# Routing batch 0 inside the last heads of a sandwich of attention and mixture of experts

## The chip, the cores and the metric

The kernel runs on 1 core of one Trainium2 chip. The metric is the device time of one execution in microseconds; a lower number is better. The core has TensorE (matmuls, written PE), VectorE (DVE), ScalarE (ACT), GpSimd (POOL) and SyncE (SP), which runs no arithmetic here and issues most DMA transfers. The engines run their own instruction streams in order and wait for each other by semaphores.

## The reference

Two layers with residuals. The input is x of 2 batches, 1024 tokens, width 128.

```python
x = x + layernorm(attention(layernorm(x)))
x = x + layernorm(moe(layernorm(x)))

# attention: 16 heads of 64, causal, relative bias clipped at 127 steps,
# logits / 64, softmax, out @ Wo + bo
# moe, over N = 2048 tokens:
shared = new_gelu(xf @ Wfc_s + bfc_s) @ Wproj_s + bproj_s      # 128 -> 512 -> 128
probs = softmax(xf @ Wr)                                       # 8 experts
topk_p, topk_i = top_k(probs, 2); topk_p /= sum(topk_p)
routed = sum over e of (new_gelu(xf @ Wfc[e] + bfc[e]) @ Wproj[e] + bproj[e]) * gate[:, e]
out = shared + routed
```

## The kernel before

Tokens lie in 16 blocks of 128 (blocks 0 to 7 are batch 0, 8 to 15 batch 1). Matrices enter TensorE split into a high and a low part, and a product is three matmuls (`three`, L1369 to L1371).

**Attention.** One head has S = 16 slots, one for each block of queries: slots 0 to 7 are batch 0, slots 8 to 15 batch 1. Such a half head is called a unit here. In a slot, TensorE computes scores (L1461), VectorE adds the bias and takes the row minimum (L1071), ScalarE takes the exponential (L817), two slots later TensorE transposes the probabilities into one of two banks trans_ps (L1476), ScalarE copies the high part out (L838), VectorE subtracts the low part (L1084). Products with V (L1494) and the output weights (L1508) are filled in at slots set by PV_SLOT and WO_SLOT. VectorE scales the head's result (`scale_head`, L1102), GpSimd adds it to `acc` (`add_head`, L626). Every engine runs `slot` for 16 slots of each head: head 0 written out, heads 1 to 14 as a loop (`Fori(1, H - 1)`), head 15 written out, and then the slots from S to TAIL that finish it. In slots GpSimd also splits the projection weights of the next head (`split_wqk`), splits V, and prepares one half of an expert's weights per head (`split_half`, stored by SyncE to `split_scratch`).

**Behind attention.** For each batch of 8 blocks: moments of `acc` (`moments`), an inverse root (`root` on GpSimd, three Newton steps on VectorE), the residual sum (`add_normed`), moments again, normalising on ScalarE (`normalise_moe_in`), transposes and evacuation (`nT_evac`), router logits, exponential, the choice of two experts (`choose`), the rank of every token within its expert by matmuls with a triangle of ones (`ranks`), and slot numbers (`find_slots`). With these GpSimd scatters each token's row (its 128 values, its gate, its number) twice into `rows_scratch`: `dispatch(b)` issues 16 indirect transfers for a batch, one per block and choice. `find_tiles` makes the table of 23 tiles of 256 rows. SyncE waits for the table, loads the first four tiles' weights, waits for all scatters (`dispatched`), and loads rows. TensorE meanwhile works on the shared expert: `hidden_units(0, c, 0)` and `second_layer(0, c, 0)` for four column groups c, in blocks of 12 wide matmuls, then `turn_shared`. Then the tiles follow (`tile_in`, `tile_units`, `tile_second`, `tile_result`), each result scattered by GpSimd, and last the sums, the layer norm and the output.

## Time and profile before

| | us |
|---|---|
| median of 3 runs | 793.9 (791.12 to 797.13) |
| the profiled execution, its own time | 788.15 |
| its span | 786.4 |
| busy: TensorE, VectorE, ScalarE, GpSimd | 697.0, 626.8, 551.9, 336.6 |

The page cuts the span into 40 slices and gives each engine's busy share in tenths. The timeline gives single instructions in order of time, with the idle time ahead of one and what ended it in brackets; "remote" and "issue" there mean that the profile shows no releaser. Times in the text are microseconds from the start of this span. The part of the span up to about 60 us loads and projects, attention runs from there to about 582, the routing and the shared expert to about 670, the tiles to about 760, the end sums to 786.

### The profile page before, as it was taken

How to read it: one execution, taken by the hardware profiler on the slowest of the kernel's cores; microseconds unless marked ns; L12 is line 12 of the kernel's file. 1: busy time of each engine (PE TensorE's matmuls, PEld its weight loads, DVE VectorE, ACT ScalarE, POOL GpSimd, SP SyncE). 2: the span in 40 equal slices, each digit the busy share in tenths (PEclk: the TensorE clock that was granted, in tenths of full speed). 3: DMA queues.
4: the chain of work that ended last, by engine and by line, in shares of the span. 5: the costliest groups of instructions: out<-in, count | busy, mean ns of one | idle time of the engine just before them, and what ended most of it. 6: DMA issues, size and time to landing. Idle time of an engine off the chain costs nothing.

```text
span 786.4 us, 17200 instructions
## 1 busy us (share of the span) xinstructions
PE 697.0 (89%) x4466; PEld 614.5 (78%) x4466; DVE 626.8 (80%) x1663; ACT 551.9 (70%) x1305; POOL 336.6 (43%) x417
## 2 busy tenths in 40 slices
PE   5978999999999999999999999999976566899930
PEld 4857888888888888888888888888875444899920
DVE  5648888889888898888988888888888615688837
ACT  2437888788887888888888888878724414888823
POOL 2518864243432434334343343333343770156544
PEclk9979999999999999999999999999997677999985
DMA  8683653546436465364553645536300246599823
GB/s 297 240 301 79 162 137 83 152 86 170 131 73 161 89 158 137 67 164 93 151 137 72 158 98 146 137 80 157 105 2 1 60 145 212 196 354 370 287 84 110
DMA packets 81474, 114.85 MB, mean 146 GB/s; under 512 B 42432, under 2 KB 59328, under 8 KB 79008
## 3 DMA queue, kind: packets, MB, share of 16 engines
q1 hardware_dynamic: 78656, 108.71, 49.6%
q0 software_dynamic: 2496, 5.15, 1.8%
q10 hardware_dynamic: 288, 0.59, 0.3%
q8 instruction: 14, 0.23, 0.1%
q14 instruction: 20, 0.16, 0.1%
HBM read 48.32 MB, written 32.56 MB: 103 GB/s over the span
## 4 chain that ended last, share of the span: by engine, by line
PE 72%; DVE 9%; issue 6%; DMA 3%; POOL 3%; another core or an unknown queue 3%; ACT 3%; SPq 0%; ACTq 0%; POOLq 0%; DVEq 0%
PE out_ps L1494 17%; PE score_ps L1461 16%; PE trans_ps L1476 16%; PE shared_ps L1508 7%; PE shared_ps L1369 2%; DVE pT_lo L1316 2%; PE shared_ps L1371 2%; PE shared_ps L1370 2%; PE score_ps L1371 2%; PE score_ps L1369 2%; PE score_ps L1370 1%; PE out_ps L1410 1%; DMA v_scratch<-probs 1%; PE trans_ps L1369 1%
## 5 line engine op out<-in xcount | busy, mean ns | idle before, releaser
L817 ACT ACTIVATE probs<-score_ps,row_min 128x128 f32<-128x128 f32 (+7 forms) x256 | 189.8, 742 | 54.1 <-DVE row_min L1071 54.0
L1084 DVE TENSOR_TENSOR pT_lo<-trans_ps,pT_hi 128x512 fp32r<-128x512 f32 (+3 forms) x384 | 201.6, 552 | 17.1 <-ACT pT_hi L838 17.0
L838 ACT ACTIVATE pT_hi<-trans_ps 128x512 fp32r<-128x512 f32 (+3 forms) x384 | 185.0, 491 | 41.2 <-PE trans_ps L1476 29.4
L1071 DVE CUSTOM_DVE_ANT_0 score_ps<-score_ps,bias 128x128 f32<-128x128 f32 (+7 forms) x256 | 194.7, 760 | 22.4 <-PE score_ps L1461 19.2
L1476 PE MATMUL trans_ps<-ident,probs 128*128 128x128 f32 x1152 | 190.9, 275 | 2.3 <-DVE pT_lo L1084 1.6
L1461 PE MATMUL score_ps<-k_hl,q_hl 128*128 128x512 f32 (+2 forms) x768 | 184.3, 354 | 2.4 <-DMA k_hl<-k_hl 1.3
L626 POOL TENSOR_TENSOR acc<-acc,head_out 128x512 f32<-128x512 f32 x64 | 83.1, 1298 | 215.9 <-DVE head_out L1102 215.8
L1476 PEld LDWEIGHTS trans_ps<-ident,probs 128*128 128x128 f32 x1152 | 137.3, 140 | 26.6 <-DVE pT_lo L1084 12.2
L1494 PE MATMUL out_ps<-pT_hi,v_hl 128*128 128x512 f32 (+2 forms) x384 | 156.5, 409 | 1.1 <-DVE pT_lo L1084 1.1
L1461 PEld LDWEIGHTS score_ps<-k_hl,q_hl 128*128 128x128 f32 x768 | 135.8, 190 | 23.4 <-issue 2.0
L1494 PE MATMUL out_ps<-pT_lo,v_hl 128*128 128x512 f32 (+2 forms) x384 | 133.0, 347 | 0.0
L1494 PEld LDWEIGHTS out_ps<-pT_hi,v_hl 128*128 128x128 f32 x384 | 72.7, 189 | 5.5 <-DVE pT_lo L1084 1.3
L1494 PEld LDWEIGHTS out_ps<-pT_lo,v_hl 128*128 128x128 f32 x384 | 73.3, 191 | 4.4
L1508 PE MATMUL shared_ps<-wo,oT 128*128 (+1 forms) x512 | 70.0, 275 | 0.8 <-ACT oT L846 0.8
L1508 PEld LDWEIGHTS shared_ps<-wo,oT 128*128 128x128 f32 x512 | 65.7, 191 | 3.5 <-issue 1.0
L1028 DVE TENSOR_TENSOR k_hl<-shared_ps,k_hl 128x512 fp32r<-128x512 f32 x64 | 44.2, 691 | 28.2 <-ACT k_hl L781 28.2
L612 POOL CAST v_hl<-v_raw 128x512 fp32r<-128x512 f32 x32 | 19.6, 611 | 90.6 <-PE out_ps L1494 69.1
L817 ACT ACTIVATION_READ_ACCUMULATOR probs<-score_ps,row_min 128x1 f32 x256 | 51.9, 203 | 0.0
L1316 DVE TENSOR_TENSOR pT_lo<-probs,pT_hi 128x256 fp32r<-128x256 f32 x92 | 38.9, 424 | 11.7 <-issue 4.6
L958 ACT ACTIVATE probs<-score_ps,tile_bias 128x256 f32<-128x256 f32 x92 | 41.9, 475 | 7.9 <-PE score_ps L1371 4.9
L1102 DVE TENSOR_TENSOR head_out<-shared_ps,row_inv 128x512 f32<-128x512 f32 x64 | 42.3, 661 | 1.1 <-PE shared_ps L1508 1.0
L614 POOL TENSOR_TENSOR v_hl<-v_raw,v_hl 128x512 fp32r<-128x512 f32 x32 | 41.1, 1284 | 2.7
(246 smaller groups left out, 1177.2 us busy)
## 6 DMA issues: line engine op xcount, KB each, us to landing
q_hl<-k_hl SPq DMA_DIRECT2D x64, 256.0 KB, 3.7
k_hl<-k_hl SPq DMA_DIRECT2D x32, 512.0 KB, 4.5
v_scratch<-probs SPq DMA_DIRECT2D x16, 512.0 KB, 4.2
v_raw<-v_scratch SPq DMA_DIRECT2D x32, 256.0 KB, 4.1
split_scratch<-normed_rows SPq DMA_DIRECT2D x16, 512.0 KB, 5.3
k_hl<-split_scratch SPq DMA_DIRECT2D x16, 512.0 KB
rows_scratch<-wv SPq DMA_DIRECT2D x16, 455.0 KB, 6.3
normed_rows<-in_W_halves SPq DMA_DIRECT2D x16, 256.0 KB, 3.8
```

The costliest lines, as they stand in the source:

```text
L626: pool.tensor_tensor(acc[:, blocks, :], acc[:, blocks, :], head_out[c][:].rearrange("p (t d) -> p t d", d=D), ALU.add)\
L817: act.activation(probs[s % 4][:, 0:n], scores_of(s % QB)[:, 0:n], ACT.Exp, bias=row_min[:, s:s + 1], scale=-1.0, accum_out=row_sum[:, s:s ...
L838: act.activation(pT_hi[c][:, CH * g:CH * g + m, q * P:(q + 1) * P], trans_ps[k % 2][:, 0:m * P].rearrange("p (m q) -> p m q", q=P), ACT.Co ...
L1028: dve.tensor_tensor(k_hl[b][:, 1, cols], shared_ps[:], k_hl[b][:, 0, cols], ALU.subtract).then_inc(qk_lo, 1)
L1071: dve.tensor_tensor_reduce(out=ps, in0=ps, in1=bias_b[b][:, T - n:T], scale=1.0, scalar=3e38, op0=ALU.add, op1=ALU.min, accum_out=row_min[ ...
L1084: dve.tensor_tensor(pT_lo[c][dst], trans_ps[k % 2][:, 0:m * P].rearrange("p (m q) -> p m q", q=P), pT_hi[c][dst], ALU.subtract).then_inc(p ...
L1102: dve.tensor_tensor(head_out[c][:].rearrange("p (t d) -> p t d", d=D), shared_ps[:].rearrange("p (t d) -> p t d", d=D), row_inv[:, blocks] ...
L1316: dve.tensor_tensor(lo, raw, hi, ALU.subtract).then_inc(tile_lo, 1)
L1461: last = pe.matmul(scores_of(i)[:, at:end], q, k_hl[b][:, part, at:end], start=part == 0, stop=part == 1)
L1476: last = pe.transpose(trans_ps[k % 2][:, o:o + P], probs[s % 4][:, j * P:(j + 1) * P], ident[:])
L1494: last = pe.matmul(out_ps[:, q0:W], v_hl[b][:, j, :], part[c][:, j, q0:W], start=j == 0 and part is pT_hi, stop=j == nk - 1 and part is pT_lo)
L1508: last = pe.matmul(shared_ps[:, j * P:(j + 1) * P], oT[c][:, j * P:(j + 1) * P], wo[:, h, :], start=True, stop=True)
```

## The change

The first eight heads stay as they are (both batches in a head). The last eight are taken batch by batch: loop heads 8 to 11 run batch 0 of heads 8 to 15, two in each, and loop heads 12 to 15 run batch 1 of them (`unit`). So batch 0's attention is complete when loop head 12 begins, and its routing is laid into the 64 slots of loop heads 12 to 15 by a function `route_early(z)` on each engine, z being the slot 0 to 63. Heads 7 to 15 are now written out instead of looped. 13 of batch 0's 16 scatters stand in slots 55 to 63, the other 3 right behind the last slot. Batch 1 is routed behind attention in two groups, blocks 8 to 11 and 12 to 15 (PICKS). The projection weights are split once for each unit of the last eight heads. The shared expert's weights become two more of the halves that are split in the heads (18 instead of 16; two heads take two), and are loaded once in the last head. Two blocks of shared hidden units are moved ahead of batch 1's routing. Tokens are numbered by partition first, which makes the loads of tile rows (1040 bytes a piece instead of 520) and of the results (2048 instead of 512) longer pieces.

```diff
+    LAST = 8
+    F = H - LAST
+    P0 = F + LAST // B
+    TWICE = (F + 1, F + 2)
+    SCATTERS = {55: 1, 56: 2, 57: 2, 59: 1, 60: 2, 61: 2, 62: 2, 63: 1}
+    EARLY = sum(SCATTERS.values()) - QB
+    PICKS = [(0, QB), (QB, QB + CH), (QB + CH, NB)]
...
+    def unit(h, b):
+        if isinstance(h, int) and h >= F:
+            i = B * (h - F) + b
+            return F + i % LAST, i // LAST
+        return h, b
...
+            # GpSimd
+            def add_residual(c):
+                blocks = slice(CH * c, CH * (c + 1))
+                pool.wait_ge(std_ready, c + 1)
+                then_wait(pool.tensor_tensor(acc[:, blocks, :], acc[:, blocks, :],
+                                             rstd[:, blocks].unsqueeze(2).broadcast_to([P, CH, D]), ALU.mult))
+                pool.tensor_tensor(x_sb[:, blocks, :], x_sb[:, blocks, :], acc[:, blocks, :], ALU.add).then_inc(residual_added, 1)
...
+                if z in (10, 11):
+                    root(1, CH * (z - 10), CH * (z - 9))
+                if z in (14, 15):
+                    add_residual(z - 14)
+                if z in (18, 19):
+                    root(2, CH * (z - 18), CH * (z - 17))
+                if z == 24:
+                    name_rows(0)
...
+                for n in range(SCATTERS.get(z, 0)):
+                    k = sum(m for y, m in SCATTERS.items() if y < z) + n
+                    dispatch(0, k // QB, k % QB)
...
-            with pool.Fori(1, H - 1) as h:
+            with pool.Fori(1, F - 1) as h:
                 for s in range(S):
                     slot(h, s, True, False)
-            for s in range(S):
-                slot(H - 1, s, True, True)
+            for h in range(F - 1, H):
+                for s in range(S):
+                    slot(h, s, True, h == H - 1)
...
+            # ScalarE
+                if 22 <= z < 22 + QB:
+                    normalise_moe_in(z - 22, z - 21)
+                if z in (29, 37):
+                    nT_evac(1, (z - 29) // 8)
+                if z == 46:
+                    exp_logits(0)
...
-            exp_logits(0)
-            normalise_moe_in(1)
-            for c in range(NC, NCH):
-                nT_evac(1, c)
+            hidden_units(0, 0)
+            normalise_moe_in(QB, QB + CH)
+            nT_evac(1, NC)
+            act.wait_ge(moe_in_ready, QB + CH)
             copy_rows(1)
             exp_logits(1)
-            hidden_units(0, 0)
+            normalise_moe_in(QB + CH, NB)
+            nT_evac(1, NC + 1)
+            act.wait_ge(moe_in_ready, NB)
+            copy_rows(2)
+            exp_logits(2)
             hidden_units(0, 1)
...
+            # VectorE
+                if z in (9, 10):
+                    lo = CH * (z - 9)
+                    if z == 9:
+                        dve.wait_ge(acc_added, P0 * B * NC)
+                    moments(acc, lo, lo + CH)
+                if z in (12, 13):
+                    lo = CH * (z - 12)
+                    stand(lo, lo + CH).then_inc(std_ready, 1)
+                if z in (17, 18):
+                    lo = CH * (z - 17)
+                    dve.wait_ge(residual_added, z - 16)
+                    moments(x_sb, lo, lo + CH)
+                if z in (20, 21):
+                    lo = CH * (z - 20)
+                    scale_and_offset(2, lo, lo + CH)
+                if z == 24:
+                    make_order()
+                if z in (29, 37):
+                    nT_evac(1, (z - 29) // 8)
+                if z == 45:
+                    take_logits(0)
+                if z in (47, 49):
+                    choose(0, (z - 47) // 2)
+                if z == 51:
+                    share(0)
+                if z == 53:
+                    find_slots(0)
...
+            # TensorE
+                if z in (28, 36):
+                    wait_shared(h, s, last)
+                    transposes(1, (z - 28) // 8)
+                if z in (30, 38):
+                    pe.wait_ge(nT_ready, NCH + 1 + (z - 30) // 8)
+                if z == 44:
+                    wait_shared(h, s, last)
+                    logits(0)
+                if z == 46:
+                    pe.wait_ge(logit_ready, 1)
+                if z == 52:
+                    wait_shared(h, s, last)
+                    ranks(0)
+                if z == 54:
+                    pe.wait_ge(ranks_taken, 1)
...
-            keep_busy(56)
-            for c in range(NC):
-                transposes(1, c)
-            pe.wait_ge(wo_scaled, H * B * NC)
-            pe.wait_ge(nT_ready, NCH + NC)
-            logits(0)
-            pe.wait_ge(wfc_ready, 1)
-            hidden_units(0, 0, 0)
+            hidden_units(0, 1, 0)
+            keep_busy(24, trans_ps[1])
+            transposes(1, NC)
+            pe.wait_ge(nT_ready, NCH + NC + 1)
+            logits(1)
+            transposes(1, NC + 1)
+            ranks(1)
+            pe.wait_ge(nT_ready, 2 * NCH)
+            logits(2)
             keep_busy(16, trans_ps[0])
-            ranks(0)
-            for c in range(NC, NCH):
-                transposes(1, c)
-            pe.wait_ge(nT_ready, 2 * NCH)
-            logits(1)
-            ranks(1)
-            hidden_units(0, 1, 0)
+            ranks(2)
             second_layer(0, 0, 0)
```

The comments that name an engine are added here. `hidden_units(0, 0, 0)` now stands on TensorE in slot 18 of the last head, ahead of the last products with V.

**GpSimd from the end of the last head to the tiles.** `rstd<-var_eps,minus_half` is `root`, `rows_scratch<-` are scatters. Before, behind the last `split_half` and `move_empty`:

```order
L559 TENSOR_SCALAR normed_rows<-normed_rows 128x2
L626 TENSOR_TENSOR acc<-acc,head_out 128x512
L712 TENSOR_SCALAR normed_rows<-token 128x16
L712 TENSOR_SCALAR bias_all<-token 128x16
L736 CAST wqk_hl<-wr 128x8
L737 TENSOR_TENSOR wqk_hl<-wr,wqk_hl 128x8
L577 TENSOR_TENSOR rstd<-var_eps,minus_half 128x8
L626 TENSOR_TENSOR acc<-acc,head_out 128x512 x2
L577 TENSOR_TENSOR rstd<-var_eps,minus_half 128x8 x2
```

Then four rows that split the shared weights, one more root, and the scatters:

```order
L577 TENSOR_TENSOR rstd<-var_eps,minus_half 128x8
L724 DMA rows_scratch<-normed_rows,slot_u 18432x130 x8
L724 DMA rows_scratch<-bias_all,slot_u 18432x130 x8
L724 DMA rows_scratch<-normed_rows,slot_u 18432x130 x8
L724 DMA rows_scratch<-bias_all,slot_u 18432x130 x8
```

Now, the part in the last head and right behind it:

```order
L693 DMA rows_scratch<-wqk,slot_u 18432x130 x5
L603 CAST normed_rows<-normed_rows 128x512
L606 TENSOR_TENSOR normed_rows<-normed_rows 128x512
L661 TENSOR_TENSOR acc<-acc,head_out 128x512
L593 TENSOR_SCALAR wv<-wv 128x7
L593 TENSOR_SCALAR normed_rows<-normed_rows 128x2
L693 DMA rows_scratch<-wqk,slot_u 18432x130 x3
L693 DMA rows_scratch<-bias_all,slot_u 18432x130 x4
L661 TENSOR_TENSOR acc<-acc,head_out 128x512
L693 DMA rows_scratch<-bias_all,slot_u 18432x130 x4
L661 TENSOR_TENSOR acc<-acc,head_out 128x512
L611 TENSOR_TENSOR rstd<-var_eps,minus_half 128x4
```

and behind the last statistics:

```order
L661 TENSOR_TENSOR acc<-acc,head_out 128x512
L611 TENSOR_TENSOR rstd<-var_eps,minus_half 128x4
L671 TENSOR_SCALAR normed_rows<-token 128x8
L671 TENSOR_SCALAR bias_all<-token 128x8
L611 TENSOR_TENSOR rstd<-var_eps,minus_half 128x4 x2
L693 DMA rows_scratch<-normed_rows,slot_u 18432x130 x4
L693 DMA rows_scratch<-bias_all,slot_u 18432x130 x4
L693 DMA rows_scratch<-normed_rows,slot_u 18432x130 x4
L693 DMA rows_scratch<-bias_all,slot_u 18432x130 x4
```

16 of 32 scatters have moved ahead of GpSimd's last two additions, 13 of them into the slots, and 16 stand behind the last roots.

**VectorE in slots 3 to 6 of the last head** (z = 51 to 54). L1071 and L1145 are the row minimum with its read-out, L1084 and L1158 the low part of the transposed probabilities. Before:

```order
L1102 TENSOR_TENSOR head_out<-shared_ps,row_inv 128x512
L1071 ISA score_ps,row_min<-score_ps,bias 128x640
L1071 ISA row_min 128x1
L1084 TENSOR_TENSOR pT_lo<-trans_ps,pT_hi 128x3x128
L1071 ISA score_ps,row_min<-score_ps,bias 128x768
L1071 ISA row_min 128x1
L1084 TENSOR_TENSOR pT_lo<-trans_ps,pT_hi 128x4x128
L1071 ISA score_ps,row_min<-score_ps,bias 128x896
L1071 ISA row_min 128x1
L1084 TENSOR_TENSOR pT_lo<-trans_ps,pT_hi 128x4x128
```

Now, from slot 5 on:

```order
L1145 ISA score_ps,row_min<-score_ps,bias 128x768
L1145 ISA row_min 128x1
L1158 TENSOR_TENSOR pT_lo<-trans_ps,pT_hi 128x4x128
L1268 SCALAR_TENSOR_TENSOR place<-count,shared_ps 128x64
L1274 TENSOR_TENSOR place_of<-place,pick 128x64
L1275 TENSOR_REDUCE slot_f<-place_of 128x8
L1276 CAST slot_u<-slot_f 128x8
L1274 TENSOR_TENSOR place_of<-place,pick 128x64
L1275 TENSOR_REDUCE slot_f<-place_of 128x8
L1276 CAST slot_u<-slot_f 128x8
L1145 ISA score_ps,row_min<-score_ps,bias 128x896
L1145 ISA row_min 128x1
```

The seven rows of `find_slots(0)` stand between the subtraction of slot 5 and the row minimum of slot 6. Eleven more such insertions stand in earlier slots of the last four heads.

## Rows read from the trace of the kernel before

**Rows 1.** The page: busy tenths of TensorE and GpSimd in 40 slices of the span.
```profile
PE   5978999999999999999999999999976566899930
...
POOL 2518864243432434334343343333343770156544
```

**Rows 2.** Stages: window us, busy us (instructions) by engine, clock, DMA share, GB/s.
```profile
476.00:508.50 32.50, 32.49 (x215) 28.83 (x213) 28.70 (x69) 26.96 (x65) 12.64 (x17) 1.00 0.50 123
...
587.00:609.70 22.70, 13.70 (x79) 11.62 (x77) 19.23 (x97) 9.96 (x23) 8.64 (x7) 0.77 0.00 1
...
626.00:655.00 29.00, 13.85 (x36) 9.36 (x36) 4.92 (x10) 3.63 (x7) 18.98 (x20) 0.73 0.41 124
655.00:670.50 15.50, 13.02 (x52) 9.76 (x52) 11.72 (x30) 9.62 (x18) 0.00 (x0) 0.84 0.87 282
670.50:750.00 79.50, 75.97 (x618) 73.39 (x619) 65.86 (x196) 66.14 (x181) 38.85 (x38) 1.00 0.84 293
```

**Rows 3.** Timeline in one head: start us, us, engine line op, shapes, [idle before <-releaser].
```profile
484.59 0.69 DVE L1084 TENSOR_TENSOR pT_lo<-trans_ps,pT_hi 128x512 fp32r<-128x512 f32 x1
...
485.40 0.60 PE L1476 MATMUL trans_ps<-ident,probs 128*128 128x128 f32 x4
...
485.75 1.10 DVE L1071 CUSTOM_DVE_ANT_0 score_ps<-score_ps,bias 128x896 f32<-128x896 f32 x1 [0.46 <-PE score_ps L1461]
```

**Rows 4.** Timeline of GpSimd: the first and the last of 32 scatters.
```profile
609.71 1.25 POOL L724 DMA_INDIRECT rows_scratch<-normed_rows,slot_u  x1 [7.35 <-DVE slot_u L1248]
...
649.82 0.95 POOL L724 DMA_INDIRECT rows_scratch<-bias_all,slot_u  x1 [0.30 <-issue]
```

**Rows 5.** Timelines of ScalarE, SyncE and TensorE during the scatters.
```profile
621.89 0.69 ACT L913 ACTIVATE probs<-score_ps,layer_bias_T 128x512 f32<-128x512 f32 x1 [2.04 <-PE score_ps L1371]
626.10 0.69 ACT L913 ACTIVATE probs<-score_ps,layer_bias_T 128x512 f32<-128x512 f32 x1 [3.52 <-PE score_ps L1371]
...
632.43 0.69 ACT L913 ACTIVATE probs<-score_ps,layer_bias_T 128x512 f32<-128x512 f32 x1 [5.13 <-remote]
...
654.99 1.26 ACT L913 ACTIVATE probs<-score_ps,layer_bias_T 128x512 f32<-128x512 f32 x2 [15.05 <-remote]
...
628.78 3.52 SPq L476 DMA_DIRECT2D k_hl<-split_scratch  x2
...
650.56 0.59 PE L1371 MATMUL trans_ps<-pT_hi 128*128 128x512 f32 x1 [2.41 <-issue]
```

**Rows 6.** Timeline of TensorE behind attention.
```profile
580.93 1.13 PE L1508 MATMUL shared_ps<-wo,oT 128*128 128x128 f32 x8 [0.78 <-ACT oT L846]
...
601.87 0.43 PE L1369 MATMUL score_ps<-nT_hi,pT_hi 128*128 128x512 f32 x1
...
604.70 1.91 PE L1410 MATMUL trans_ps<-ident 128*128 128x128 f32 x16
...
606.93 0.92 PE L1612 MATMUL shared_ps<-taken,ones 128*128 128x56 f32 x7
...
619.86 0.77 PE L1369 MATMUL score_ps<-nT_hi,pT_hi 128*128 128x512 f32 x1
...
670.54 0.41 PE L1639 MATMUL out_ps<-ident,wqk 128*128 128x128 f32 x2 [0.29 <-ACT acc L936]
```

**Rows 7.** Timeline of VectorE: moments, inverse root, and first and last routing operation.
```profile
777.14 0.87 DVE L999 BATCH_NORM_STATS2 stats<-acc 128x6 f32<-128x128 f32 x4
...
778.46 0.17 DVE L1004 TENSOR_SCALAR var_eps<-mv 128x4 f32<-128x4 f32 x1
...
775.13 0.15 DVE L1010 TENSOR_TENSOR newton<-rstd 128x4 f32<-128x4 f32 x1
...
775.74 0.16 DVE L1145 SCALAR_TENSOR_TENSOR offset<-mv,rstd 128x4 f32<-128x4 f32 x1
...
603.69 0.21 DVE L1218 TENSOR_REDUCE top<-rank 128x8 f32<-128x64 f32 x1
...
609.24 0.17 DVE L1248 CAST slot_u<-slot_f 128x8 uint32<-128x8 f32 x1
```

563 lines of the change are left out of this document (308 added, 255 removed).

## The prediction

> **What bounds the kernel now.** I read the page first. TensorE is busy in every slice of the attention stretch and thins out to 5 to 8 tenths in slices 30 to 35; in slices 32 and 33 GpSimd, little used in attention, is busier than TensorE [rows 1]. The table by stage says it in numbers: a head takes 32.50 us, TensorE is busy for all of it and VectorE for 28.70, so VectorE has 3.8 us to spare per head. Behind attention TensorE is half idle: from 587 to 609.7 VectorE is the busiest engine, from 626 to 655 no compute engine is; from 655 to 670.5 TensorE catches up, and from 670.5 on run the 23 expert tiles, where it is full again [rows 2].
>
> Next the timelines. In a head, the transposes of one slot start at 485.40, just 0.12 us after VectorE's subtraction of two groups earlier ends (484.59 + 0.69); TensorE's transposes take turns in two banks that VectorE frees. VectorE itself then waits 0.46 us for scores [rows 3]. So the two engines pull on each other, and work given to VectorE in such slots soon comes out at TensorE.
>
> Behind attention GpSimd issues 32 scatters of rows, one each 1.265 us, from 609.71 to past 649.82 [rows 4]. In the last two thirds of them the others crawl: a gelu at 621.89 is still in time, the next ones come at 626.10 and 632.43, and after one more (6.3 us on) at 654.99; SyncE needs 3.5 us to issue two transfers; TensorE stands 2.41 us between two matmuls of one sum, which wait for nobody [rows 5]. All recover once the scatters have ended. The shared expert's matmuls are what is late: the first transpose of the first tile is at 670.54 [rows 6].
>
> **The change part by part.** The sum is made against the profiled execution: 788.15 us, of which the span is 786.4. It lies 5.75 us below the median of the runs, 793.9, and I carry that difference over.
>
> *Added to attention.* The routing of batch 0 now runs in the slots of the last four heads. On VectorE it is: moments of four blocks (777.14 to 778.63, say 1.4 us) four times, the inverse root with its last product (775.13 to 775.90, say 0.8) four times, and about 0.8 us of small operations for the order, 9.6 us together in slots 9 to 24. Then two evacuations of 0.65 us in slots 29 and 37. Then 0.9 us for the logits, four operations like those in the row of 603.69, and 5.7 us from the first choice to the last slot number (603.69 to 609.41), 6.6 us in slots 45 to 53 [rows 7]. Each of the three clusters is covered only by VectorE's spare time in its own slots. Of the 3.8 us per 16 slots I count 0.8 as usable, since part of it is wait for a neighbour [rows 2, 3]: 9.6 less 3.0, 1.3 less 0.9, and 6.6 less 1.8, together about 12. TensorE itself gets 8 transposes, 16 narrow matmuls and 8 more for the ranks, about 4 us at the 0.12 us that its narrow matmuls take (seven in 0.92) [rows 6]; 3 of these stand beside the third cluster, 1 adds. The attention stretch grows by 13 us. The bounds are 5 (if the slack of two slots by which the softmax runs ahead takes up most) and 18 (if no spare time is usable and TensorE's 4 us add).
>
> Nothing is charged for the rest. ScalarE gets 8 normalisations (about 0.4 us each) and two copies in 27 slots and has 5.5 us to spare per head; GpSimd's extra splits of the projection weights and its two residual additions stand in 19.9 us of spare time per head [rows 2]. If GpSimd were late, the values' matmuls would wait next. The shared weights cost one load in the last head instead of a load and four operations behind it, which were hidden.
>
> *The scatters.* 13 of batch 0's 16 stand in slots 55 to 63, 3 right behind. That is 16.5 us in about 18 us, and GpSimd has some 5 us of other work there, so it runs late by 3 to 4 us, and its last addition but one is needed about 8 us behind the last slot: just covered. By the Trainium skill (SBUF — State Buffer, Who interferes with whom) a scatter of GpSimd's is held up while VectorE runs a two-port operation, from about 0.62 to 3.1 us in its example. The rows of the tile stage, where VectorE is busy for 65.86 of 79.5 us, have 38 scatters in 38.85 us, 1.02 each [rows 2], which is as long as the row of 649.82, where VectorE idles [rows 4]; with the pitch I take 1.265.
>
> *Behind attention.* I walk the new order with the same durations, in times of the profile of before, without the 13 us. One block of shared hidden units goes ahead of the last values, so the last output product moves from 580.93 to 582.4 [rows 6]. Batch 1 goes in groups of four blocks: statistics of group 1 at 582, its sum at 586.6, the second statistics at 589.4, normalised by ScalarE at 593.8, turned and evacuated at 596.5, logits at 598.6, exponential at 600.2 (ScalarE now has to load its table twice more, because gelu goes ahead). Group 2's normalisation is queued behind that exponential and its evacuation ahead of group 1's choice: choice at 604.2 to 607.2, the slots of group 1 at 612 (before, batch 0's were ready at 609.4). Group 2 chooses until 615, has its slots at 617.5 and the tile table at 621. GpSimd scatters 16 times from 612: 20.2 us, to 632, against 650.8 before [rows 4]. TensorE's remaining six blocks wait for VectorE, which splits the first hidden units only behind the table, about 624. A block of 12 wide matmuls took 2.83 us at a granted clock of 1.00 (601.87 to 604.70) and 5.1 at half clock (from 619.86) [rows 6]. One at 4.4 and five at 2.9 with 0.8 us between them end at 644; four turns of 0.7 us, 647; and 2.5 us for slow issue late in the 16 scatters (it began about 12 us into the 32). The first tile starts at 649.5 instead of 670.5: 21 us earlier. Bounds: 14 (the chain of group 1 is 7 us longer) and 27 (no slow issue, full clock). The tiles take the 91 us that they took. Rows are now loaded and summed in longer pieces, for which I take 1.5 us off the end, between 0 and 3.
>
> **Sum.** +13 - 21 - 1.5 = -9.5: profiled 778.7, and 784.4 beside the median.
>
> **Rivals.**
> - *A, the slots absorb it.* If the softmax's lead of two slots hides the clusters, attention grows by 5 to 7 us: 793.9 + 6 - 21 - 1.5 = 777.5. For it: the first clusters stand just behind the first slots of a batch, where blocks are short. Against: the margin of 0.12 us [rows 3].
> - *B, batch 1's own chain is long.* Two groups cost two passes over each wait, and ScalarE's order (hidden units, normalise, exponential, normalise) puts group 2 behind group 1. If the first scatter of batch 1 is 7 to 10 us later than I have it, the tiles start only 12 us earlier: 793.9 + 13 - 12 - 1.5 = 793.4, no change. For it: every one of some 20 hand-overs between engines in this chain is counted here at its bare duration.
> - *C, the scatters stop the last head; slower.* In before, slow issue set in about 12 us into an unbroken run of scatters [rows 5]. In the last head TensorE needs over six matmuls per us, so slow issue there is a full stop. If it sets in from the tenth scatter, 7.6 us are lost (6 x 1.265): 792. If from the first, 20 us: 804.6, slower. It decides at about 9.5 us lost. Against: 38 scatters in the tile stage at a like density stop nobody [rows 2].
> - *D, VectorE holds the scatters up.* If each of the 16 waits for one more of VectorE's operations of about 1.1 us [rows 3], 17.6 us are added ahead of the last two additions, of which some 14 are on the path: 798. The skill's rule (named above) goes this way; at its 3.1 us for each scatter the same sum would be over 805. The trace so far speaks against it.
>
> **How the numbers follow.** My forecast has 0.50, A 0.20, B 0.16, C 0.10, D 0.04. The predicted time is the likeliest, 784.4; its own range is 778 to 790. The whole range, 773 to 798, takes in A, B, and the milder part of C. About 1% is what a measurement of this kernel can tell from no change: 786.0 to 801.8. Of my own case six tenths lie below 786, A wholly, B hardly: faster 0.52. The rest of my case, B, and half of C: same 0.41. Slower 0.07.
>
> **What would show it.** In the profile of after: heads 8 to 11 keep 32.5 us; the last four are together 13 us longer than 130, with TensorE waiting for VectorE's pT_lo in slots 9 to 24 of them and 45 to 55; GpSimd's scatters last about 1.0 us with pitch 1.265 and TensorE isn't idle during them in the last head; from attention's last output product to the first tile about 67 us instead of 90; gelus 1.1 us apart except in the last few us of scatters. I am wrong if the last four heads grow by under 8 or over 18 us, if the span between attention and the first tile shrinks by under 15, or if the tile stage is longer because its weights come later against its start.

## Result, and the profile after

| | kernel before, us | changed kernel, us |
|---|---|---|
| median (7 runs each) | 793.9 (791.12 to 797.13) | 800.47 (798.72 to 803.4) |
| ratio of the medians | 1 | 1.0084, 95% interval 1.0062 to 1.0107 |
| the profiled execution, its span | 786.4 | 801.5 |
| first row minimum of loop head 2 | 116.8 | 117.8 |
| last output product | 580.93 | 609.64 |
| first tile | 670.54 | 677.63 |
| first to last tile | 73.9 | 81.7 |
| last tile to the end | 42.0 | 42.2 |

The change is slower by 0.8%. The forecast was 1.2% faster. From head 2 on, the way to the last output product grew by 27.8 us (491.9 against 464.1), the way from there to the first tile shrank by 21.6 us (68.0 against 89.6), and the tiles took 7.9 us longer in this one execution. The two profiled executions are no typical pair: that of the changed kernel (803.4) is 2.9 us above its median, that of the kernel before (788.15) 5.75 us below.

The page of the changed kernel, the rows that answer to [rows 1]: TensorE's thin stretch is four slices (31 to 34) instead of six (30 to 35), but slices 24, 25 and 28 to 30, in and right behind the last heads, show eights, and GpSimd's peak is split in two, one at the end of attention and one ahead of the tiles.

```profile
PE   4967999999999999999999988998887557989830
POOL 2418853343343442444434364443284170345444
```

Stages of the changed kernel, with the columns of [rows 2]: loop heads 11 to 15, the way from the last row minimum to the last output product, and the way from there to the first tile.

```profile
411.49:444.18 32.69, 32.51 (x213) 28.84 (x213) 28.96 (x69) 26.84 (x64) 13.33 (x18) 1.00 0.51 125
444.18:480.49 36.31, 33.39 (x213) 28.86 (x213) 32.80 (x95) 26.93 (x64) 18.05 (x24) 1.00 0.53 129
480.49:519.43 38.94, 34.26 (x217) 29.11 (x217) 33.84 (x106) 30.31 (x73) 18.17 (x24) 1.00 0.42 103
519.43:558.71 39.28, 36.63 (x242) 32.31 (x241) 32.61 (x81) 29.03 (x68) 15.93 (x21) 1.00 0.43 105
558.71:592.57 33.86, 30.14 (x183) 25.69 (x184) 29.51 (x80) 22.18 (x55) 14.41 (x16) 0.95 0.33 99
592.57:609.64 17.07, 13.46 (x74) 11.30 (x74) 6.70 (x15) 6.14 (x13) 11.92 (x12) 0.90 0.18 58
609.64:677.63 67.99, 41.36 (x184) 32.33 (x184) 43.63 (x170) 27.34 (x49) 21.72 (x23) 0.75 0.35 112
```

The same three last stages of the kernel before:

```profile
539.22:569.07 29.85, 28.75 (x185) 24.87 (x185) 25.13 (x62) 23.32 (x57) 9.65 (x11) 1.00 0.39 106
569.07:580.93 11.86, 9.15 (x61) 7.84 (x62) 9.34 (x30) 5.71 (x12) 4.79 (x7) 1.00 0.06 18
580.93:670.54 89.61, 56.85 (x259) 45.06 (x259) 52.14 (x206) 30.17 (x57) 41.86 (x41) 0.75 0.31 98
```

Heads 12 to 15 are 3.8, 6.4, 6.8 and 4.0 us longer (against 32.50 and 29.85), 21.0 together. VectorE is busy 3.8, 4.9, 3.7 and 4.4 us longer in them (against 28.96 in loop head 11 and 25.13 in the last head of before), 16.8 together. The stretch behind the last row minimum is 5.2 us longer. Heads 7 to 11 add 1.5.

Who waited for whom in about one head of the kernel before (474 to 506 us; us in total, times, longest), and behind it the same in loop head 13 of the changed kernel:

```profile
ACT probs L817 <- DVE row_min L1071: 3.2, 6, 1.1
DVE k_hl L1028 <- ACT k_hl L781: 1.6, 4, 0.5
...
DVE score_ps L1071 <- PE score_ps L1461: 1.1, 3, 0.5
DVE pT_lo L1084 <- ACT pT_hi L838: 0.9, 4, 0.3
```

```profile
ACT probs L878 <- DVE row_min L1145: 7.5, 9, 2.6
...
PE score_ps L1583 <- ACT probs L878: 1.4, 1, 1.4
...
PE trans_ps L1598 <- DVE pT_lo L1158: 1.3, 2, 0.8
PE trans_ps L1598 <- ACT probs L878: 1.1, 2, 0.6
```

Before, VectorE's three waits for ScalarE and TensorE make 3.6 us, nearly all of its idle time. Now TensorE waits for VectorE mainly in two ways: directly for pT_lo (1.3 us), as the forecast had it, and over ScalarE (2.5 us), whose exponentials wait 7.5 us for late row minima.

The runs were made in seven groups, each on one chip with its own runs of the kernel before, and only kernels of one group are compared by time. The groups differ: in two of them (e1 to e4; e13 to e16) the kernel before took 773 us, in the other five 791 to 795. I call them the 773 groups and the 790 groups. The experiments show where those 20 us lie. "Slow issue" is what [rows 5] show: during a run of scatters the other engines stop for microseconds with no releaser in the profile.

### The profile page after: what moved, and what is told of

It reads as the page before. It is cut to its first block, busy times and chain, and to the rows that moved or that the text cites. A ratio compares the mean times of both kernels' runs of the same rounds, so it can differ in the third digit from the quotient of the medians.

```text
span 801.5 us, 15822 instructions
## 1 busy us (share of the span) xinstructions
PE 692.9 (86%) x4435; PEld 607.2 (76%) x4435; DVE 632.2 (79%) x1704; ACT 553.2 (69%) x1308; POOL 349.5 (44%) x444
## 4 chain that ended last, share of the span: by engine, by line
PE 66%; DVE 16%; ACT 5%; DMA 5%; issue 4%; POOL 3%; SPq 0%; another core or an unknown queue 0%; ACTq 0%; DVEq 0%; POOLq 0%
PE out_ps L1616 15%; PE trans_ps L1598 14%; PE score_ps L1583 13%; PE shared_ps L1630 6%; DVE score_ps L1145 2%; PE shared_ps L1489 2%; DMA v_scratch<-probs 2%; PE score_ps L1491 2%; PE trans_ps L1489 2%; DVE pT_lo L1158 2%; PE shared_ps L1491 2%; DVE pT_lo L1436 2%; PE shared_ps L1490 2%; PE score_ps L1489 2%; PE score_ps L1490 1%
## 5 line engine op out<-in xcount | busy, mean ns | idle before, releaser
L1158 DVE TENSOR_TENSOR pT_lo<-trans_ps,pT_hi 128x512 fp32r<-128x512 f32 (+3 forms) x384 | 202.5, 553 | 22.6 <-ACT pT_hi L899 19.0
L1145 DVE CUSTOM_DVE_ANT_0 score_ps<-score_ps,bias 128x128 f32<-128x128 f32 (+7 forms) x256 | 194.6, 760 | 21.4 <-PE score_ps L1583 17.3
L1598 PEld LDWEIGHTS trans_ps<-ident,probs 128*128 128x128 f32 x1152 | 136.7, 141 | 42.2 <-issue 17.7
L1616 PEld LDWEIGHTS out_ps<-pT_lo,v_hl 128*128 128x128 f32 x384 | 73.9, 192 | 4.4
L1630 PE MATMUL shared_ps<-wo,oT 128*128 128x128 f32 (+1 forms) x512 | 70.0, 275 | 0.8 <-ACT oT L907 0.8
L1436 DVE TENSOR_TENSOR pT_lo<-probs,pT_hi 128x256 fp32r<-128x256 f32 x92 | 38.6, 424 | 19.8 <-ACT pT_hi L1025 11.3
L907 ACT ACTIVATE oT<-out_ps 128x512 f32<-128x512 f32 x64 | 38.4, 601 | 6.0 <-PE out_ps L1616 6.0
```

The source lines that it names most:

```text
L1145: dve.tensor_tensor_reduce(out=ps, in0=ps, in1=bias_b[b][:, T - n:T], scale=1.0, scalar=3e38, op0=ALU.add, op1=ALU.min, accum_out=row_min[ ...
L1158: dve.tensor_tensor(pT_lo[c][dst], trans_ps[k % 2][:, 0:m * P].rearrange("p (m q) -> p m q", q=P), pT_hi[c][dst], ALU.subtract).then_inc(p ...
L1436: dve.tensor_tensor(lo, raw, hi, ALU.subtract).then_inc(tile_lo, 1)
L1598: last = pe.transpose(trans_ps[k % 2][:, o:o + P], probs[s % 4][:, j * P:(j + 1) * P], ident[:])
L1616: last = pe.matmul(out_ps[:, q0:W], v_hl[b][:, j, :], part[c][:, j, q0:W], start=j == 0 and part is pT_hi, stop=j == nk - 1 and part is pT_lo)
L1630: last = pe.matmul(shared_ps[:, j * P:(j + 1) * P], oT[c][:, j * P:(j + 1) * P], wo[:, unit(h, b)[0], :], start=True, stop=True)
```

## Experiments

### Routing taken out of the slots

`e1_routed_behind` keeps the new order of heads. All pieces of `route_early` and the scatters run behind the last output product. One part of the result differs in it: the first block of shared hidden units is computed ahead of batch 0's normalised input, from the old operand; the work is the same.

```diff
-        return B * QB * (h - P0) + s if isinstance(h, int) and h >= P0 else -1
+        return -1
```

> The changed kernel with its new order of heads, but all of batch 0's routing and its 16 scatters stand behind the last output product instead of in the slots. In the profile of the changed kernel the last output product starts at 609.64 us (before: 580.93); by head, heads 12 to 15 grew by 21.0 us, heads 8 to 11 by 1.4. Theory (the growth is the routing laid into the slots): heads 12 to 14 fall back to 32.5 each, the last product starts at 587 (within 2 us), and only the moved block of hidden units (3.9 us) and 1 to 2 us of heads 8 to 11 are left of the growth. Rival (written-out heads or the order batch by batch cost by themselves): heads 12 to 14 stay above 34 each and the last product starts past 595. The routing is then serial: about 27 us of it come behind attention, so the time is 805 to 815 by the theory.

Measured: last product at 586.58, time 815.9 (ratio 1.0569 to the kernel before), just past the top of the 805 to 815 expected. Heads 12 to 14 take 32.7 to 32.9 and head 15 takes 29.82:

```profile
445.20:477.90 32.70, 32.51 (x213) 28.84 (x213) 28.93 (x69) 26.87 (x64) 13.34 (x18) 1.00 0.51 124
...
543.46:573.28 29.82, 28.71 (x185) 24.85 (x185) 25.17 (x61) 23.33 (x57) 9.67 (x11) 1.00 0.45 131
573.28:586.58 13.30, 11.70 (x73) 10.04 (x74) 6.11 (x12) 5.72 (x12) 2.55 (x2) 1.00 0.01 2
```

So all but 0.7 of the 21 us in heads 12 to 15 are the routing in the slots, and neither written-out heads nor the order batch by batch. (e2 below, of the same group and with the routing in the slots, has 149.6 us in these four heads, e1 128.1.) Those leave 1.6 us in heads 7 to 11, and the hidden block leaves 1.4 (13.30 against 11.86).

### What a microsecond in a slot costs

`e3_price_list` and `e8_price_list_2` are the kernel before, heads written out, with one extra piece of work in single heads.

```diff
+                n = {(2 + i, i): 6 for i in range(QB)}.get((h, s), 0)
+                if h == 14 and s % QB in (2, 3, 4):
+                    n = 3
+                for t in range(n):
+                    last = dve.bn_stats(stats[:, t, :], x_sb[:, t, :])
```

> The kernel before with all heads written out and one extra piece in single heads: six bn_stats of 128x128 on VectorE (0.22 us each, 1.3 us) behind slot i of head 2 + i, for i = 0 to 7; sixteen narrow matmuls on TensorE in slot 12 of head 11; eight transposes in slot 12 of head 13; eighteen bn_stats in threes behind slots 2, 3, 4, 10, 11, 12 of head 14; nothing extra in heads 1, 10, 12. Period of a head without extra: 32.5. Theory (margins of the two transpose banks: 0.1 to 0.3 us for blocks 5, 6, 7, 0, 1 and 1.4 to 1.8 for blocks 2 to 4, two slots behind their row minimum): 1.3 us cost 1.0 to 1.3 where the margin is narrow and 0 to 0.3 behind slots 3 to 5, the spread ones cost under 1.5 of 3.9; TensorE's pieces cost all they last, 3.6 to 4.0 for the narrow matmuls (0.25 each) and 2.1 for the transposes (0.27 each). Rival (the lead of the softmax hides pieces of this size): every VectorE piece costs under 0.4, the narrow matmuls about 2, as taken in the forecast (0.12 each).

> The kernel before with all heads written out (32.68 us each without extra) and one extra piece in single heads: ScalarE three copies of 128x128 in slot 1 of head 2 and one in each of slots 1 to 6 of head 4; GpSimd eight products of 128x128 in slot 4 of head 6 (about 0.46 us each); VectorE thirteen dependent products of 128x64 in slot 1 of head 8 (about 3.3 us), two bn_stats in slot 6 of head 12 (0.45 us), twelve bn_stats in slot 1 of head 14 (2.7 us). In the first list 1.35 us of bn_stats cost 0.85 to 1.6 and eighteen spread ones (4.05 us) 3.4. Theory (in a head TensorE and VectorE are one chain without usable slack, ScalarE and GpSimd have some): VectorE's pieces cost 0.3 to 0.5, 2.5 to 3.0 and 3.0 to 3.4; ScalarE's cost under 0.5 and under 1.0, GpSimd's under 0.5. Rival (every engine that hands over between slots is as tight): ScalarE's 1.2 and 2.4 us cost 1.0 and 2.0.

Some heads of e3: the first two without extra (10, 12), then head 2 (six bn_stats behind slot 0), head 11 (sixteen narrow matmuls), head 13 (eight transposes) and head 14 (eighteen bn_stats, spread). The first number is the period of the head.

```profile
389.12:421.80 32.68, 32.50 (x213) 28.82 (x213) 28.95 (x69) 26.89 (x64) 12.61 (x16) 1.00 0.51 125
...
456.53:489.22 32.69, 32.51 (x213) 28.82 (x213) 28.95 (x69) 26.91 (x64) 12.66 (x16) 1.00 0.46 112
```

```profile
118.16:152.33 34.17, 32.81 (x213) 28.72 (x213) 30.30 (x75) 27.19 (x64) 12.64 (x16) 1.00 0.48 119
...
421.80:456.53 34.73, 34.54 (x229) 30.49 (x229) 28.96 (x69) 27.01 (x64) 12.64 (x16) 1.00 0.51 128
...
489.22:522.80 33.58, 33.39 (x222) 29.60 (x221) 28.89 (x70) 27.01 (x64) 12.62 (x16) 1.00 0.52 128
522.80:558.86 36.06, 34.37 (x213) 28.70 (x213) 32.37 (x88) 26.59 (x64) 12.61 (x16) 1.00 0.47 116
```

And of e8: head 4 (six copies on ScalarE), head 6 (eight products on GpSimd), head 8 (thirteen dependent products on VectorE).

```profile
183.48:216.55 33.07, 32.62 (x213) 28.65 (x212) 28.89 (x69) 28.13 (x70) 12.56 (x16) 1.00 0.52 131
249.23:282.22 32.99, 32.80 (x214) 28.97 (x214) 28.88 (x70) 27.05 (x65) 15.78 (x24) 1.00 0.51 125
314.82:350.78 35.96, 33.13 (x214) 28.73 (x214) 31.79 (x83) 26.73 (x64) 12.62 (x16) 1.00 0.46 113
```

| extra piece | its length, us | head longer by, us |
|---|---|---|
| VectorE, 6 bn_stats behind slot 0, 1, ... 7 | 1.35 | 1.5, 1.6, 1.2, 1.2, 0.9, 1.0, 1.2, 1.0 |
| VectorE, 18 bn_stats spread over six slots | about 4 (3.4 more busy) | 3.4 |
| VectorE, 2 bn_stats; 12 bn_stats; 13 dependent products | 0.4; 2.4; 2.9 more busy | 0.35; 2.4; 3.3 |
| TensorE, 16 narrow matmuls; 8 transposes | 2.0; 0.9 more busy | 2.05; 0.9 |
| ScalarE, 3 copies in one slot; 6 in six slots | 0.7; 1.3 more busy | 0.0; 0.4 |
| GpSimd, 8 products of 128x128 | 3.1 more busy | 0.3 |

My theory of e3 was mostly wrong: the margins of single blocks don't matter, work behind slots 3 to 5 costs nearly as much as elsewhere (0.9 to 1.2), and TensorE's pieces cost half of what I expected. The rival, that the lead hides pieces of this size, is wrong for every piece on VectorE. A microsecond of VectorE costs 0.9 on average in the eight single places (0.6 to 1.2), and 0.8 to 1.1 in the other pieces, spread or not; ScalarE's costs a third at most, GpSimd's a tenth. Differences of 0.3 us are at the limit of this measurement: head 3 of e8, without an extra piece, is 0.26 us longer than the others too. TensorE's narrow matmuls cost 0.13 each, as the forecast had them.

`e10_small_ops_off` uses this in the changed kernel: the Newton steps, shift and offset of batch 0 run on GpSimd (`norm`, in slots 12 and 20), and so do the constants of the order.

```diff
-                if z in (12, 13):
-                    lo = CH * (z - 12)
-                    stand(lo, lo + CH).then_inc(std_ready, 1)
+                if z == 12:
+                    norm(1)
```

> The changed kernel with the Newton steps, the shift, the offset and the order's constants of batch 0 moved from VectorE (twelve to sixteen small operations in slots 12, 13, 20, 21 and 24 of the 64, 3.9 us in all) to GpSimd, which waits about 20 us per head. Theory (a us of VectorE in a slot costs 0.9 us, GpSimd's costs 0.04): loop head 12 shrinks from 36.3 by 1.0 to 1.6 us, head 13 from 38.9 by 1.8 to 2.4, together 3 to 4 us, and the last output product is as much earlier. Rival (what costs is the number of insertions and their waits, not their length): under 1.5 us in all.

```profile
445.01:480.14 35.13, 32.99 (x213) 28.74 (x213) 31.55 (x87) 26.88 (x64) 17.40 (x28) 1.00 0.54 133
480.14:517.83 37.69, 34.21 (x217) 29.07 (x217) 32.25 (x88) 30.01 (x74) 21.49 (x41) 1.00 0.43 104
```

Only 2.8 us left VectorE (32.80 to 31.55 and 33.84 to 32.25), less than the 3.9 I had counted; the two heads shrank by 2.4, 0.86 per microsecond, which is the price. The last head took 0.6 to 0.9 us more than in the other kernels (34.77 against 33.9 to 34.1); why is open. Time 797.6 (ratio 1.0049, 1.0017 to 1.0081, to the kernel before); this interval overlaps those of the changed kernel, so only the two heads show the gain.

### The scatters in the last head

`e2_scatters_out` and, in another group, `e11_scatters_out_2` put batch 0's 16 scatters behind the last roots.

```diff
+    SCATTERS = {}
...
-            for g in range(1, len(PICKS)):
+            for g in range(len(PICKS)):
```

> The changed kernel with batch 0's 16 scatters taken out of the last head and put where GpSimd waited 17 us for batch 1's slot numbers (behind its last roots). All the rest stays. Theory A (the cluster of VectorE and TensorE work makes the last head long, scatters cost little): last output product within 1.5 us of 609.6, last head 33 to 34 us. Theory B (scatters slow the others' issue in the last head too, as forecast rival C had it): last product 4 to 8 us earlier. In both, batch 1's scatters end near 661 us less what is won, with issue slow for up to 20 us ahead of that: 796 to 803.

> The kernel of e2_scatters_out again, since the two groups of runs differ by 18 us in the kernel before. From the last row minimum to the last output product the changed kernel took 17.1 and 18.2 us, e2_scatters_out 13.3. Theory (the scatters stop the last transposes and not the group of runs): 13.3 again, 4 to 5 us won in attention. Where slow issue is present it now falls into 32 scatters in a row: way from last product to first tile 75 us or more instead of 66.8, time 2 to 8 us longer than the changed kernel; where absent, 64 us.

| from last row minimum to last product, us | scatters in the last head | scatters out |
|---|---|---|
| 790 groups | 17.07 (changed kernel), 18.16 (e5), 15.38 (e10) | 13.31 (e11) |
| 773 groups | 13.30 (e15) | 13.30 (e2, and e1) |

In a 773 group the scatters cost nothing, in a 790 group 2 to 5 us (2.1 in e10, 3.8 and 4.9 in the changed kernel). ScalarE in the changed kernel, first profile, waiting for transposes; behind it the same in e15_changed_pauses (below), which has the same 16 scatters there:

```profile
596.75 0.60 ACT L899 ACTIVATE pT_hi<-trans_ps 128x512 fp32r<-128x512 f32 x1 [1.40 <-PE trans_ps L1598]
598.22 0.49 ACT L899 ACTIVATE pT_hi<-trans_ps 128x384 fp32r<-128x384 f32 x1 [0.88 <-remote]
601.03 0.60 ACT L899 ACTIVATE pT_hi<-trans_ps 128x512 fp32r<-128x512 f32 x1 [2.32 <-PE trans_ps L1598]
```

```profile
595.69 0.98 ACT L901 ACTIVATE pT_hi<-trans_ps 128x512 fp32r<-128x512 f32 x2
597.82 1.09 ACT L901 ACTIVATE pT_hi<-trans_ps 128x512 fp32r<-128x512 f32 x2 [1.16 <-PE trans_ps L1600]
```

In a 790 group the scatters cost more outside the head than in it: e11 has its first tile 77.8 us behind the last product (changed kernel 66.8 to 68.0) and takes 807.1 us, ratio 1.0154 (1.010 to 1.0208). e2 has 64.3 us and takes 787.6 against 773.4, ratio 1.0182 (the 796 to 803 expected were for a 790 group). Its last product is at 608.5, as theory A had it; e11's 13.31 against 17.07 shows theory B where slow issue is present.

### The two kinds of groups, the layout, the hidden block

> The changed kernel itself, on the chip of this group. The first profiles had the change at plus 28.7 us up to the last output product, minus 21.6 from there to the first tile, plus 7.9 in the tiles. In the group of runs before this one the kernel before took 773.4 instead of 793.9, and with the new layout its way from last product to first tile was 74.0 us instead of 89.6, with no stretch of slow issue. Theory (the growth in attention is the same everywhere, the gain behind it depends on slow issue): on a chip where the kernel before takes about 773, the change is slower by 14 to 20 us, its last product is 28 us later and the way to the first tile only 6 to 10 us shorter. Rival (the change moves both chips alike): ratio 1.008, 5 to 8 us slower.

> The kernel before, for its profile on this chip. By the theory of slow issue as a property of the chip or its state: gelus during the 32 scatters at 0.57 us behind one another and no gap over 9 us where this chip gives 773 us; gaps of 5 to 15 us as in the first profile where it gives 794.

> The kernel before with the new numbering of tokens alone: rows of tiles loaded in pieces of 1040 bytes, results in pieces of 2048 bytes. In the profiles the 22 tile pitches sum to 73.86 us before and 81.73 after the change. Theory (the tile stage differs by chance from run to run): sum of pitches 74 to 76, time 0 to 2 us shorter than before. Rival (the longer pieces, or the order in which rows lie, slow the loads of weights): pitches 78 to 82, time 4 to 8 us longer.

`e4_layout_only` changes three places of the kernel before (token numbering and the two loads). It ran in a 773 group: 771.9 against 773.4, ratio 0.9995 (0.9973 to 1.0016). The layout is worth nothing. e5 and e6 met a 790 group, on the same chip as e1 to e4: changed 797.7, before 791.1, ratio 1.0082 (1.0064 to 1.010), the first result again. So e5 could not test its own theory; e2 and e15, in 773 groups, do (1.0182 and 1.0209).

| | last product to first tile, us | sum of tile pitches, us |
|---|---|---|
| before, 790 groups | 89.6 and 89.8 (e6) | 73.9, 75.1 |
| changed, 790 groups | 68.0 and 66.8 (e5) | 81.7, 74.5 |
| before, 773 groups | 74.0 (e4), 74.6 (e3) | 71.0, 72.8 |
| changed with edits, 773 groups | 64.3 (e2), 67.2 (e15) | 71.0, 70.2 |

So the kernel before loses 15.6 us here to slow issue (89.6 against 74.0), which only the 790 groups have. Without it the changed order is 6.8 us (e15, whose pauses lengthen it) to 9.7 us (e2) shorter than 74.0, so 12 to 15 of the 21.6 us that the change won behind attention are slow issue avoided. ScalarE between the scatters, e6 and then e4:

```profile
626.61 0.69 ACT L913 ACTIVATE probs<-score_ps,layer_bias_T 128x512 f32<-128x512 f32 x1 [3.56 <-PE score_ps L1371]
...
632.93 0.69 ACT L913 ACTIVATE probs<-score_ps,layer_bias_T 128x512 f32<-128x512 f32 x1 [5.12 <-remote]
...
656.18 1.27 ACT L913 ACTIVATE probs<-score_ps,layer_bias_T 128x512 f32<-128x512 f32 x2 [14.34 <-remote]
```

```profile
624.01 0.69 ACT L912 ACTIVATE probs<-score_ps,layer_bias_T 128x512 f32<-128x512 f32 x1 [0.59 <-PE score_ps L1370]
...
635.54 1.39 ACT L912 ACTIVATE probs<-score_ps,layer_bias_T 128x512 f32<-128x512 f32 x2 [8.13 <-PE score_ps L1370]
...
641.08 1.39 ACT L912 ACTIVATE probs<-score_ps,layer_bias_T 128x512 f32<-128x512 f32 x2 [1.44 <-PE score_ps L1370]
```

TensorE in the first profile of the kernel before, between two matmuls of the shared expert:

```profile
639.47 0.79 PE L1369 MATMUL score_ps<-nT_hi,pT_hi 128*128 128x512 f32 x1 [4.63 <-issue]
```

In that profile the queues that load instructions (kind instruction, q8 and q14 on the page) moved nothing from 610 to 665 us; nor did they in e6 from 611 to 667:

```profile
q1 hardware_dynamic: 2877, 4.99, 29.9%
q0 software_dynamic: 1024, 2.13, 11.4%
```

These are all queues with packets in that stretch, so a late load of instructions is not what stops the engines. What stops them is open.

The scatters themselves have the same pitch in both (1.265). In e4 the shared expert is done before the scatters end, and the first tile waits for its rows. The tiles of the two kinds differ too. TensorE, the DMA share and GB/s (last column) in 40 us of tiles, e6 and then e4:

```profile
695.00:735.00 40.00, 38.64 (x313) 37.01 (x312) 33.71 (x101) 32.23 (x89) 22.55 (x22) 1.00 1.03 362
```

```profile
680.00:720.00 40.00, 40.00 (x343) 40.00 (x342) 36.08 (x110) 36.54 (x99) 23.31 (x25) 1.00 1.04 397
```

`e7_hidden_block_back` moves `hidden_units(0, 0, 0)` behind the last output product.

> The changed kernel with the first block of shared hidden units back behind the last output product. Theory (the block stands in TensorE's way and pays nothing back where the scatters bound the start of the tiles): last product 3 to 4 us earlier, first tile 3 to 4 us earlier, time 3 to 4 us shorter than the changed kernel. Rival (TensorE waits there anyway for the last transposes): last product at most 1 us earlier, time the same or longer by the block.

The stretch behind the last row minimum is 16.5 us instead of 18.2 (e5, same group), the way to the first tile 66.3 instead of 66.8, the time 796.8 against 797.7: the block costs 1.5 us, not 3 to 4, and taking it out is no gain that this run can tell.

> The three edits together: small operations on GpSimd, batch 0's scatters behind the last roots, first hidden block behind the last product. Theory (they add up): last output product 3.5 + 4.5 + 1.5 = 9.5 us earlier than the changed kernel's, against e11 5 us earlier. Compared with the kernel before: plus 9 us where slow issue is absent (e2 was plus 14), and about plus 2 where it is present. Rival (they overlap): last product no more than 6 us earlier.

`e12_three_together` took 804.5 against e11's 807.1. The stretch behind the last row minimum fell to 11.86, exactly that of the kernel before, but heads 13 and 15 didn't shrink (39.2 and 35.1). From head 2 to the last product it took 487.3, against 488.7 in e11: 1.4 us, not 5. The edits don't add up, and against the kernel before e12 is 11.4 us slower, where I had expected 2. Why head 15 grew is open.

### Pauses between the scatters

All four kinds are the kernel before, but for e15, with something behind some scatters:

```diff
                         pool.indirect_dma_start(...)
+                        if t % 4 == 3 and (b, i, t) != (1, 1, NB - 1):
+                            then_wait(pool.tensor_scalar(head_out[0][:], head_out[0][:], 1.0, None, ALU.mult))
```

That is e9. e13 and e17 do the same on 4 columns instead of 512, e14 and e18 the long one behind every eighth scatter, e16 waits there for all scatters so far instead, and e15 has the long one behind every fourth of batch 1's 16.

> The kernel before with one operation of GpSimd on 128x512 (about 1.3 us, its result unused) behind every fourth of the 32 scatters, seven in all. Slow issue was there in the groups of runs where the kernel before took 791 and 794 us, and absent where it took 773. Theory A (an unbroken run of scatters brings slow issue on): with pauses it goes away or starts later, gelus stay under 3 us apart, the scatters end 9 us later, and where slow issue is present the first tile starts 5 to 8 us earlier than 671.7. Theory B (pauses of that size change nothing): slow issue stays and the first tile starts 0 to 9 us later; time plus 2 to 9 us. Where slow issue is absent anyway: plus 8 to 9 us.

> The kernel before with a tiny operation of GpSimd (128x4, about 0.25 us, and a wait for its end) behind every fourth of the 32 scatters, where e9_pauses had one on 128x512 (1.5 us). With e9 the scatters ended at 663.7, the shared expert's last turn was at 655.4 and the first tile at 668.0; the kernel before had 671.7. Theory A (any operation between scatters takes slow issue away): gelus 0.57 us apart, scatters end near 655, first tile 659 to 661, time 8 to 12 us less than before. Theory B (the pause must be long): gaps of 5 to 15 us as in the kernel before, first tile 671 to 674, time 0 to 3 us more. Where slow issue is absent: 2 to 4 us more in both.

> The kernel before with the long operation of e9_pauses behind every eighth scatter, three in all. In the kernel before slow issue began about 12 us, nine or ten scatters, into the run. Theory A (it is the length of an unbroken run, and eight scatters are short enough): scatters end at 655 to 657, first tile at 659 to 661, time 8 to 12 us less. Theory B (eight are too many): some slow issue ahead of each pause, first tile 663 to 670.

> The changed kernel with the same long operation behind every fourth of batch 1's 16 scatters, three in all. In the changed kernel ScalarE waited 13 to 16 us for gelus in these scatters, and the first tile was 66.8 to 68.0 us behind the last output product. Theory (slow issue still takes 5 to 8 us there, as forecast part of the walk, which charged 2.5 us): 60 to 63 us instead, time 4 to 7 us less than 797.7, about equal to the kernel before. Rival (those scatters end too late for anything else to matter, and pauses add to them): 66 to 72 us, time the same or 3 us longer.

> The kernel before in which GpSimd waits behind every eighth scatter until all scatters so far have landed (2.3 to 2.5 us from issue by the profile), three times, without an operation. Theory A (slow issue comes from scatters that pile up or from the unbroken run as such; a drain ends it like an operation does): first tile 661 to 664, time 6 to 10 us less. Theory B (an ordinary operation of GpSimd is what resets it): slow issue stays, first tile 671 to 678, time 0 to 6 us more.

> The kernel of e13_tiny_pauses again. Where slow issue is absent (the kernel before takes about 773) it was 2.5 us slower, first tile at 660.9. Where it is present (791 to 794): theory A (any operation between scatters takes it away) first tile again at 660 to 662, against 670.5 to 671.7, time 775 to 783; theory B (only the long operation of e9_pauses does) gelus 5 to 15 us apart, first tile 671 to 674, time 791 to 797.

> The kernel of e14_three_pauses again. Where slow issue is present: theory A (what matters is a long operation now and then; eight scatters in a row are short enough) no gap of ScalarE's above the 8 to 10 us that it waits for the second layer in any case, first tile 79 to 81 us behind the last output product, against 89.7 in the kernel before, time 8 to 12 us less than before. Theory B (runs of eight are too long) gaps ahead of each pause, first tile 84 to 90 us behind it, time 0 to 6 us less. Where absent: 5 us more, as e14 had.

| kernel | group: before, us | time, us | ratio (95%) | last product to first tile, us |
|---|---|---|---|---|
| e9, seven long | 793.1 | 790.6 | 0.9957 (0.9932 to 0.9982) | 85.6 |
| e18, three long | 793.4 | 784.2 | 0.9881 (0.9846 to 0.9917) | 80.4 |
| e17, seven tiny | 795.5 | 788.0 | 0.9887 (0.9821 to 0.9952) | 89.8 |
| e13, seven tiny | 773.2 | 775.6 | 1.0034 (1.0017 to 1.0051) | 78.2 |
| e14, three long | 773.2 | 778.0 | 1.0061 (1.004 to 1.0083) | 80.5 |
| e16, three drains | 773.2 | 781.8 | 1.0111 (1.0079 to 1.0143) | 82.3 |
| e15, changed kernel, three long | 773.2 | 788.8 | 1.0209 (1.0187 to 1.0232) | 67.2 |

Three or seven long operations take slow issue away where it is present (in e9 ScalarE's longest wait is 10.0 us, for TensorE). ScalarE in e18, whose gaps are those of a 773 group:

```profile
623.50 0.69 ACT L915 ACTIVATE probs<-score_ps,layer_bias_T 128x512 f32<-128x512 f32 x1 [0.59 <-PE score_ps L1373]
...
634.00 1.39 ACT L915 ACTIVATE probs<-score_ps,layer_bias_T 128x512 f32<-128x512 f32 x2 [6.74 <-PE score_ps L1373]
...
639.56 1.39 ACT L915 ACTIVATE probs<-score_ps,layer_bias_T 128x512 f32<-128x512 f32 x2 [1.46 <-DVE pT_lo L1179]
```

The first tile is then late only by the scatters' end, which three pauses move less than seven. e18 beats both kernels where the kernel before takes 793 us; in a 773 group the same three pauses cost 4.9 us. Tiny operations seem to help in part: e17's profiled execution, the longest of its four runs and 8 us above their median, has gaps of 2 to 14 us and no shorter way (the 89.8 in the table), while the median is 7 us lower than before; one profile of so long a run settles nothing. e15 and e16 met a 773 group, so whether pauses help the changed kernel, or drains anything, stays open. The changed kernel itself never ran in a 773 group. e15 comes nearest to what the change is worth without slow issue: with 67.2 us from last product to first tile, no less than where slow issue is present, it loses 15.6 us to the kernel before. If its three pauses cost what they cost in e14, 4.9 us, some 11 are left.

## Why the prediction was wrong, point by point

**Added to attention: 13 forecast, 26.4 measured** (27.8 less the hidden block's 1.4, which the forecast counts in its walk). The operations were counted right: 17.5 us on VectorE (16.8 more busy in the four heads) and 4 on TensorE (2.05 and 0.9 by the price list, and the ranks). On VectorE they stand in 16 insertions (z = 9 to 53), not in the twelve that I gave. The step that failed is "Of the 3.8 us per 16 slots I count 0.8 as usable", where 0.8 is a share: 3.0 of 3.8 us in the first cluster. Hardly any of it is. By the price of 0.9, VectorE's 16.8 us cost 15.1; with 4 on TensorE and the 0.7 that e1 leaves in these heads that makes 19.8, and 21.0 are measured; the last 1.2 us are open, and within what the single pieces spread by (0.6 to 1.2). VectorE's 3.8 idle us in a head are its waits for TensorE and ScalarE, and are not time that more work could fill. The row that I used to argue for the tight coupling, the margin of 0.12 us [rows 3], said so already; the averages [rows 2] misled me into deducting 5.7 us. The other half of the slip is plain arithmetic: the upper bound, "no spare time is usable and TensorE's 4 us add", is 17.5 + 4 = 21.5 by my own terms and not 18. "I am wrong if the last four heads grow by [...] over 18 us" was met.

**Nothing charged for the rest.** ScalarE's and GpSimd's pieces are nearly free, as forecast (0.0 to 0.4 us for pieces of 0.7 to 3.1 us). Written-out heads 7 to 11 with their new order, charged at nothing, cost 1.5.

**The scatters: "just covered" forecast, 3.8 us measured** (17.07 less 13.31), and 4.9 in e5. This is rival C in a mild form: slow issue set in behind the last slot, where transposes, ScalarE and VectorE hand over one by one. The argument against C failed: it took the tile stage for "a like density", but 38 scatters in 79.5 us are one in 2.1 us, and here they stand in runs of five, seven and four with a pitch of 1.27. In 773 groups the forecast was right, with 0.0. Rival D is out: they last 0.95 to 1.07 us each in the slots (the first 1.25), so VectorE doesn't hold them up. The Trainium skill (SBUF — State Buffer, A bandwidth-pool intuition that's wrong) has 0.62 going to 3.1 us in its example, beside a copy on VectorE; no run here shows that.

**Behind attention: 67 us from last product to first tile forecast, 68.0 and 66.8 measured.** Batch 1's first scatter came 30.0 us behind the last output product (walk: 29.6). The gain of 21 us was right, and in the groups with slow issue it was for the reason given: 32 scatters in a row became 16. In a 773 group the kernel before needs only 74, and 7 to 10 us of the gain are left.

**The tiles: same time forecast, +7.9 in the profile, 0 to 3 by the groups.** In the group of e5 to e8 the changed order has 74.5 and 76.8, the old one 75.1 and 75.2, and e4 shows that the layout costs nothing. So most of the 7.9 us was the spread of one execution. Not all of it need be: in the 790 groups the six profiles with the changed order have 74.5 to 81.7 (mean 77.6), the three with the old order and no pauses 73.9 to 75.2. I count 0. **End and rows: -1.5 forecast, 0 measured** (e4: 0.9995; last tile to the end 41.8 in e4 and in e6).

The sum with the measured terms: +26.4 - 20.2 + 0 = +6.2 (the walk being 21.6 less the block's 1.4), against 6.6 between the medians, in 790 groups. Of the 15.7 us between it and the forecast, 8.0 are the price of the slots (21.0 against 13), 3.8 the scatters in the head, 1.5 the written-out heads, 1.5 the end and 0.8 the walk. Rival A (the slots absorb it) is wrong by the price list, rival B (batch 1's chain is long) by the 30.0 us above.

## What to carry to other kernels

Where, as here, TensorE is busy throughout a loop and another engine waits for it and is waited for in every step, don't take that engine's idle time for spare time: charge work put there at its full length until a run has priced it, and price it by putting one known piece into one iteration and reading its period. Work for such a loop belongs on the engines where a piece was priced low (here GpSimd, and ScalarE for pieces up to 1.3 us). A gain that comes from avoiding a bad stretch (slow issue) is better taken by breaking up the stretch itself: three pauses won 9 us in a 790 group where moving the routing lost 6.6.
